# First-layer weights loaded once in 16 rows, and the first chunk joined to the first pair's transfer in a factorization-machine kernel

## The reference

```python
x_reg = input_data @ W_lin.T + b_lin
emb = input_data @ factors
sum_squared = jnp.square(emb.sum(axis=1))
squared_sum = (jnp.square(input_data) @ jnp.square(factors)).sum(axis=1)
h = jax.nn.relu(emb @ W1.T + b1)          # 16 -> 128
h = jax.nn.relu(h @ W2.T + b2)            # 128 -> 64
dnn_out = h @ W3.T + b3                   # 64 -> 1
x = x_reg + 0.5 * (sum_squared - squared_sum)[:, None] + dnn_out
x = 0.5 + jax.nn.sigmoid(x) * 5.0
```

## Time and profile before

| | us |
|---|---|
| median of 3 runs (lowest, highest) | 133.63 (133.58, 133.83) |
| the profiled execution | 133.64 |
| its span, first to last instruction | 131.8 |
| TensorE matmul busy | 107.9 (82%) |
| ScalarE busy | 61.4 (47%) |
| VectorE busy | 52.6 (40%) |
| mean DMA rate over the span | 397 GB/s |

### The profile page before, as it was taken

The page is one execution under the profiler, slowest core; times in us unless marked ns, Lnnn a source line. Parts: engine busy times, 40 slices in busy tenths (PEclk is TensorE's granted clock), DMA queues, the critical chain, the costliest instruction groups (busy, mean ns, idle before and its releaser), DMA issues.

```text
span 131.8 us, 2604 instructions
## 1 busy us (share of the span) xinstructions
PE 107.9 (82%) x1123; PEld 34.9 (26%) x1123; DVE 52.6 (40%) x51; ACT 61.4 (47%) x52; POOL 17.6 (13%) x48
## 2 busy tenths in 40 slices
PE   6059989439999739969649979999569997989992
PEld 4012222012222112212112233222022222345881
DVE  0391063036036036045045016564065351576571
ACT  4030067039039039049058046867069571465851
POOL 3015000200046200110200110064200400000000
PEclk9999999965899977999986999999999999999999
DMA  4999999999999999999999999999999999999700
GB/s 116 417 519 408 408 457 462 398 408 477 428 408 432 447 427 398 467 437 408 437 447 427 398 467 447 393 437 437 398 413 428 438 415 422 414 405 412 304 25 1
DMA packets 3201, 52.36 MB, mean 397 GB/s; under 512 B 372, under 2 KB 504, under 8 KB 1400
## 3 DMA queue, kind: packets, MB, share of 16 engines
q1 hardware_dynamic: 3192, 52.23, 93.2%
HBM read 52.22 MB, written 0.00 MB: 396 GB/s over the span
## 4 chain that ended last, share of the span: by engine, by line
DMA 53%; PE 42%; SPq 1%; DVE 1%; issue 1%; ACT 1%
DMA xr<-in_x_pairs 37%; PE p_lin L506 36%; DMA xr<-in_x_end 16%; PE p_sq L506 2%; PE p_h L600 2%; PE p_tot L506 1%; PE p_h L631 1%; DVE h L454 0%; DVE h L449 0%; PE p_tot L613 0%; SPq L273 0%; SPq L267 0%; SPq L266 0%; ACT lin L341 0%; PE p_tot L620 0%
## 5 line engine op out<-in xcount | busy, mean ns | idle before, releaser
L327 ACT ACTIVATE sq<-xr 128x2560 f32<-128x2560 f32 x20 | 45.8, 2332 | 45.6 <-DMA xr<-in_x_pairs 42.7
L427 DVE TENSOR_TENSOR sq<-xr 128x1536 f32<-128x1536 f32 x20 | 34.6, 1765 | 53.4 <-DMA xr<-in_x_pairs 48.8
L506 PE MATMUL p_lin<-xr,wr 128*17 128x512 f32 x320 | 42.4, 674 | 13.6 <-DMA xr<-in_x_pairs 13.6
L506 PE MATMUL p_lin<-sq,wz 128*18 128x512 f32 x320 | 36.5, 592 | 0.0
L506 PEld LDWEIGHTS p_lin<-xr,wr 128*17 128x17 f32 x320 | 9.6, 107 | 44.3 <-issue 37.6
L307 POOL COPY wr<-hd 128x136 f32 (+1 forms) x20 | 9.6, 482 | 77.8 <-PE p_lin L506 77.8
L506 PEld LDWEIGHTS p_lin<-sq,wz 128*18 128x18 f32 x320 | 9.9, 98 | 24.8 <-issue 24.7
L506 PE MATMUL p_lin<-xr,hd 128*17 128x352 f32 (+1 forms) x128 | 10.0, 380 | 1.3 <-DMA xr<-in_x_end 1.3
L506 PE MATMUL p_lin<-x_one,hd 32*17 32x256 f32 (+1 forms) x28 | 6.1, 654 | 4.4 <-DMA x_one<-in_x_first 4.4
L437 DVE TENSOR_TENSOR sq<-xr 128x1408 f32<-128x1408 f32 (+3 forms) x6 | 6.6, 1134 | 6.1 <-DMA xr<-in_x_end 6.1
L337 ACT ACTIVATE sq<-xr 128x1408 f32<-128x1408 f32 (+3 forms) x6 | 5.7, 982 | 6.3 <-DMA xr<-in_x_end 6.3
(11 more groups left out here) (50 smaller groups left out, 39.5 us busy)
## 6 DMA issues: line engine op xcount, KB each, us to landing
xr<-in_x_pairs SPq DMA_DIRECT2D x9, 4096.0 KB, 21.9
xr<-in_x_groups SPq DMA_DIRECT2D x2, 2048.0 KB, 17.6
xr<-in_x_end SPq DMA_DIRECT2D x1, 2112.0 KB, 17.4
xr<-in_x_end SPq DMA_DIRECT2D x3, 640.0 KB, 19.0
xr<-in_x_end SPq DMA_DIRECT2D x1, 1760.0 KB, 21.2
xr<-in_x_end SPq DMA_DIRECT2D x1, 1056.0 KB, 16.2
hd<-in_head SPq DMA_DIRECT2D x1, 952.0 KB, 4.8
x_one<-in_x_first SPq DMA_DIRECT2D x1, 896.0 KB, 6.6
```

The costliest lines, as they stand in the source:

```text
L327: nc.scalar.activation(sq[:, ring(s), BY_DVE:CHUNKS, :], xr[:, s, BY_DVE:CHUNKS, :], ACT.Square).then_inc(act_squared, 1)
L427: nc.vector.tensor_tensor(sq[:, ring(s), 0:BY_DVE, :], xr[:, s, 0:BY_DVE, :], xr[:, s, 0:BY_DVE, :], ALU.mult).then_inc(dve_squared, 1)
L506: return nc.tensor.matmul(out, lhsT, rhs, start=False, stop=False, skip_group_check=True)
```

## The change

W1 no longer stands in hd: hd's parameter part loses 128 columns (512 bytes in each of 128 rows, 64 KB). A new input w1_once of 16 rows by 256 columns (16 KB) carries W1 transposed beside four identity blocks; one matmul spreads it over the four quarters into a PSUM bank, VectorE copies it into a tile w1, and the first layer reads that. Its transfer stands second in SP's queue.

Chunk 0, the remainder and the first pair now lie side by side in one tile x_all and come in one transfer (39,936 bytes a row), which raises x_landed[0]. All that waited for first_landed now waits for x_landed[0].

Waits: in groups 12 to 17 ScalarE and VectorE wait for a pair's landing once, and not again for its second group (six waits left out); rest_copied is waited for ahead of `square_end(7, 1)` and no longer together with p_lin_done[2].

```diff
-C_W1 = 0
-C_W2 = C_W1 + H1
+C_W2 = 0
         hd = sb("hd", [P, HD])
-        x_one = sb("x_one", [P, B + REST_SETS * REST_COLS])
-        xr = sb("xr", [P, SLOTS, CHUNKS, HALF])
+        w1_sel = sb("w1_sel", [EMB, H1 + P])
+        w1 = sb("w1", [P, H1])
+        x_all = sb("x_all", [P, FIRST + SLOTS * CHUNKS * HALF])
...
             sp.dma_start(hd[:, :], head).then_inc(hd_landed, 16)
-            sp.dma_start(x_one[:, :], x_first).then_inc(first_landed, 16)
-            for p in range(PAIRED // TWO):
+            sp.dma_start(w1_sel[:, :], w1_once).then_inc(w1_landed, 16)
+            sp.dma_start(x_all[:, 0:FIRST + TWO * CHUNKS * HALF], x_first[:, 0:FIRST + TWO * CHUNKS * HALF]
+                         ).then_inc(x_landed[0], 16)
+            for p in range(1, PAIRED // TWO):
...
-            act.wait_ge(first_landed, 16)
+            act.wait_ge(x_landed[0], 16)
             nc.scalar.activation(sqf[:, :], xf[:, :], ACT.Square).then_inc(first_squared, 1)
...
             for g in range(GROUPS, PAIRED):
-                landed(act, g // SLOTS, g % SLOTS)
+                if g % TWO == 0:
+                    landed(act, g // SLOTS, g % SLOTS)
...
-            dve.wait_ge(first_landed, 16)
+            dve.wait_ge(x_landed[0], 16)
             nc.vector.tensor_tensor(sql[:, :, :], xl[:, :, :], xl[:, :, :], ALU.mult).then_inc(rest_squared, 1)
...
+            dve.wait_ge(w1_done, 1)
+            nc.vector.tensor_copy(w1[:, :], p_h1[0][:, 0:H1]).then_inc(w1_ready, 1)
             dve.wait_ge(p_h1_done[0], 2)
...
             for g in range(GROUPS, PAIRED):
-                landed(dve, g // SLOTS, g % SLOTS)
+                if g % TWO == 0:
+                    landed(dve, g // SLOTS, g % SLOTS)
...
             square_end(7, 0)
+
+            dve.wait_ge(rest_copied, 1)
             square_end(7, 1)
-            dve.wait_ge(rest_copied, 1)
             copy_block(2)
...
             pe.wait_ge(hd_landed, 16)
-            pe.wait_ge(first_landed, 16)
+            pe.wait_ge(x_landed[0], 16)
...
             remainder(WZ, ws[:, ENDS + 1:, :], sql)
+            pe.wait_ge(w1_landed, 16)
+            nc.tensor.matmul(p_h1[0][:, 0:H1], w1_sel[:, H1:H1 + P], w1_sel[:, 0:H1],
+                             start=True, stop=True, skip_group_check=True).then_inc(w1_done, 1)
...
-                    mm = nc.tensor.matmul(bank[32 * t:32 * t + 32, 0:n], pr[:, C_W1 + 32 * t:C_W1 + 32 * t + 32], rhs,
+                    mm = nc.tensor.matmul(bank[32 * t:32 * t + 32, 0:n], w1[:, 32 * t:32 * t + 32], rhs,
...
+            pe.wait_ge(w1_ready, 1)
             layer1(0)
```

More of the change, by code:

```diff
@@ L45 @@
 REST_COLS = B // (P // REST_K)
+FIRST = B + REST_SETS * REST_COLS
 BY_DVE = 3
@@ L83, with fm_kernel @@
 HD = HD_L + REST_SETS * LIN
-def fm_kernel(nc, head, x_first, x_pairs, x_groups, x_end, out):
+def fm_kernel(nc, head, w1_once, x_first, x_pairs, x_groups, x_end, out):
     with ExitStack() as ctx:
@@ L120, in fm_kernel @@
         warm = sb("warm", [P, 1])
-        xf = x_one[:, 0:B]
-        xl = x_one[:, B:].rearrange("p (c b) -> p c b", b=REST_COLS)
+        xf = x_all[:, 0:B]
+        xl = x_all[:, B:FIRST].rearrange("p (c b) -> p c b", b=REST_COLS)
+        xr = x_all[:, FIRST:].rearrange("p (s c b) -> p s c b", s=SLOTS, c=CHUNKS)
         w = hd[:, 0:HD_P].rearrange("p (c k) -> p c k", k=LIN)
@@ L135, in fm_kernel @@
         hd_landed = sem("hd_landed")
-        first_landed = sem("first_landed")
+        w1_landed = sem("w1_landed")
+        w1_done = sem("w1_done")
+        w1_ready = sem("w1_ready")
         x_landed = [sem(f"x_landed{t}") for t in range(SLOTS // TWO)]
@@ L273, in _ @@
                 sp.dma_start(xr[:, at:at + TWO].rearrange("p s c b -> p (s c b)"),
-                             x_pairs[p, :, 0:TWO * CHUNKS * HALF]).then_inc(x_landed[at // TWO], 16)
+                             x_pairs[p - 1, :, 0:TWO * CHUNKS * HALF]).then_inc(x_landed[at // TWO], 16)
             for g in range(PAIRED, TOTAL):
@@ L726 @@
     x_rest = rest.reshape(REST_SETS, REST_K, P // REST_K, REST_COLS).transpose(2, 1, 0, 3).reshape(P, -1)
-    x_first = np.concatenate([xT[:P], x_rest], axis=1)
     chunks = xT[P + REST:].reshape(ALL - 1, P, B)
@@ L738 @@
             x_groups[g - PAIRED, :, :CHUNKS * HALF] = rows
+    x_first = np.concatenate([xT[:P], x_rest, x_pairs[0]], axis=1)
+    x_pairs = np.ascontiguousarray(x_pairs[1:])
     ends = chunks[ALL - 1 - ENDS:]
@@ L749 @@
     params = head[:, HD_P:HD_L]
+    w1_once = np.zeros((EMB, H1 + P), f32)
+    w1_once[:, :H1] = np.asarray(L0_rec_W1).T
     for t in range(4):
-        params[32 * t:32 * t + EMB, C_W1:C_W1 + H1] = np.asarray(L0_rec_W1).T
+        w1_once[:, H1 + 32 * t:H1 + 32 * t + EMB] = np.eye(EMB, dtype=f32)
         params[32 * t:32 * t + EMB, C_SE] = 1.0
@@ L761 @@
     params[:, C_B3] = np.asarray(L0_rec_b3)
-    arrays = {"head": head, "x_first": x_first, "x_pairs": x_pairs, "x_groups": x_groups, "x_end": x_end}
+    arrays = {"head": head, "w1_once": w1_once, "x_first": x_first, "x_pairs": x_pairs, "x_groups": x_groups, "x_end": x_end}
     nc = bacc.Bacc("TRN2", target_bir_lowering=False, num_devices=1)
```

## The result

The changed kernel took 135.11 us in the median of 22 runs (133.64 to 137.04), the kernel before 133.65 us (133.50 to 133.83, 22 runs). I had forecast 133.42. The fastest executions equal those of before; the others lie anywhere up to 3.4 us above. The ratio, 1.0039 with a 95% interval of 1.0025 to 1.0054, leaves out executions more than 1.5% above the fastest, which are 10 of the 22 here, so it tells the smaller part of the loss. What has to be explained is a scatter that before does not have. (In the changed kernel line 518 is the matmul in `add_mm`, 506 before, and line 280 the issue of a pair, 273 before. The views leave digits out of names, so w1_sel stands there as w_sel.)

A forecast was written before the change was run, and what follows sets the result against it. The stream of transfers was taken to bound the kernel. From 133.64 us, 0.14 less for the stream and 0.07 less for the moved wait made 133.43, forecast as 133.42; own range 133.25 to 133.6, 8 in 10 within 133.1 to 133.9.

The forecast's parts named there:

- Bound: Whole kernel: the stream of transfers sets the time to the last byte; a microsecond less there is one less overall.
- landings: Pairs on the DMA stream: landed at 17.59, 28.52 and 38.24 us before; merged transfer expected at 17.45.
- code packets: DMA engines: an instruction packet holds up one of 16 by about 1.2 us; a pair lands with the slowest.
- The start: Chunk 0's work waits for the merged transfer at 17.45 us; pair 0 used up at 34.0 at the latest.
- The queue stays full, by 0.6 to 1.9 us: At pair 3's issue: data flow at 35.0 to 36.3 us, before pair 2 is done at 36.9 to 38.1.
- The delay costs 0: After the later start: TensorE finishes pair 2 at 48.2 us, against pair 3 landing at about 48.1.
- a dip of the share: Sign against the forecast: the DMA share dips between 34 and 38 us.
- Rival 1: At pair 3: pair 0 used up later than about 35.5 us, the queue runs dry, likelier 133.9 us; chance 0.08.
- the 16-row transfer: W1's new transfer in SP's queue: costs 0.03 us of stream, bounds 0 to 0.06, the queue behind it being full.
- rival 3: W1's small transfer holds the DMA engines up for up to 1 us, 134.2 at half of that; chance 0.04.
- The bytes: Head of the stream: hd loses 64 KB, w1_once adds 16, so 0.11 us less stream.
- The moved wait: VectorE's addition for block 2 at the end: a single wait saves 0.07 us, bounds 0 and 0.10.

The follow-up runs named there:

- after_delay: Changed kernel with eight more matmuls of 512 columns on TensorE ahead of the W1 matmul: 135.45 us, ratio 1.0131.
- issue_late: Kernel before, with SP issuing pair 3 only when three groups are used up, not two: 135.98 us, ratio 1.0148.
- merge_warm: Kernel before with the merged transfer, the seven wait changes and 60 matmuls of zeros, W1 left in the head: 133.58 us, ratio 0.9998.
- swap_warm: Changed kernel with W1's transfer behind the merged one and 60 matmuls of zeros while TensorE waits: 133.70 us, ratio 0.9995.
- lighter: Changed kernel without the squared products of chunk 0 and the remainder, W1's transfer still ahead: 134.49 us, ratio 1.0039.
- swap: Changed kernel with the merged transfer second in SP's queue and W1's third: 134.45 us, ratio 1.0057.
- merge_18: Kernel before with the merged transfer, issued only after GpSimd's two fills (about 1.8 us), no short transfer ahead: 133.73 us, ratio 1.0017.
- merge_only: Kernel before with chunk 0, the remainder and the first pair in one transfer, W1 still in the head: 133.92 us, ratio 1.0017.
- late_start: Kernel before, transfers untouched, but ScalarE, VectorE and TensorE wait for the first pair before touching chunk 0: 134.68 us, ratio 1.0078.
- merge_twice: Kernel before with only the merged transfer, W1 still in the head, a repeat of merge_only: 133.69 us, ratio 1.0012.
- after_again: Changed kernel unchanged, timed once more: 134.81 us (133.62 to 136.73), ratio 1.0043.
- after_warm: Changed kernel with 50 matmuls of zeros while TensorE waits for the first transfer: 133.97 us, ratio 1.0029.
- split: Changed kernel with chunk 0 and the remainder in their own transfer again, W1's transfer still second: 133.84 us, ratio 1.0015.
- split_swap: Changed kernel with chunk 0 and the remainder in their own transfer, issued second, W1's third: 133.69 us, ratio 1.0004.
- waits_only: Kernel before with only the seven waits changed: 133.69 us, ratio 0.9998.

## Why the prediction was wrong

- **Bound, landings, code packets**: right. What pair 3's landing lost in after_delay and issue_late, 1.1 and 2.3 us, is in the time in full.
- **The start**: the mechanism was right and its numbers too. I had the merged transfer at 17.45 us and pair 0 used up by 34.0 at the latest; the changed kernel's two profiles have 17.51 and 17.52, and issues of pair 3 at 32.94 and 33.95.
- **The step that failed** is the one after it: "The queue stays full, by 0.6 to 1.9 us", from which "The delay costs 0" follows. I let data flow until 36.9 us and took 1 to 2.3 us from issue to data, so that only an issue later than about 35.5 would cost. All profiles that bear on it, in us:

| | pair 3 issued | pair 2 lands | pair 3 lands | execution |
|---|---|---|---|---|
| before | 24.73 | 38.24 | 48.12 | 133.64 |
| merge_warm | 31.15 | 38.16 | 47.94 | 133.64 |
| swap_warm | 32.24 | 38.14 | 48.15 | 133.77 |
| lighter | 32.33 | 38.90 | 48.79 | 134.54 |
| changed | 32.94 | 38.52 | 48.23 | 133.79 |
| swap | 33.15 | 38.04 | 48.11 | 133.75 |
| merge_18 | 33.18 | 38.45 | 48.17 | 133.86 |
| merge_only | 33.25 | 38.16 | 48.41 | 134.07 |
| late_start | 33.52 | 38.31 | 48.47 | 134.54 |
| merge_twice | 33.77 | 38.21 | 47.95 | 133.52 |
| after_again | 33.95 | 38.47 | 48.62 | 134.88 |
| after_warm | 35.57 | 38.33 | 50.19 | 135.83 |
| after_delay | 35.74 | 38.29 | 49.20 | 135.00 |
| issue_late | 36.84 | 38.48 | 50.46 | 136.12 |

  Up to 33.2 us the issue costs nothing clear (lighter's landings are all late, from the merged transfer on). From 33.25 to 33.95, up to 5 us before pair 2 has landed, it costs between nothing (merge_twice) and 0.5 us. Beyond 35.5 it costs 1.1 to 2.3. So there is no single edge at 35.5, and the loss begins some 2 us earlier.
- **Why the margin was wrong.** It was worked out from 36.9, when the slower of the engines that no code packet held up are done with pair 2; by the landings' records the first of the 16 is done at 36.0 to 36.4. That is not enough: data came 0.95 us after the issue in after_delay and issue_late, so by that an issue at 33.95 was still in time for every engine. What the sum had at nothing is that the first packets of a late transfer are slow. By the packets' records those of 32 KB around 36 us took 2.0 to 2.4 us in three cases in after_again and 1.7 to 2.2 in fourteen in after_delay, 1.21 otherwise, and in merge_twice none did. In after_delay the DMA share stayed at 0.99 while the rate fell, so the sign that I had named, a dip of the share, did not come there (in issue_late it did). Why the first packets are slow stays open. Rival 1, at 0.08, had the late issue but as a queue that runs dry.
- **What this explains of the changed kernel.** Its issue falls between 32.9 and 34 us, where the loss begins, and the rise of the clock decides where. That gives up to 0.5 us. The 10 of 22 executions at 135.8 us and above need more: a merged transfer that lands late as well, as in after_warm, a further hit at the end, as in after_again, or something that no profile shows. So the late issue is shown to cost (issue_late) and the late start to scatter (late_start); that they make up the whole loss is not shown.
- **A part of the sum that I had at 0.03 us**, the 16-row transfer, goes with a landing of the long transfer behind it that is late by over a microsecond in some executions (18.57 and 18.83 us, where the others have 17.35 to 17.68; in split 8.93 against 7.67). My reason, the full queue behind it, does not hold for the place that it has, at 1.2 us, when head's data still fill the queue alone; that this is the reason is not shown. This was rival 3, at 0.04. Where a late landing makes the issue later still, both add up: 135.83 us in after_warm's profile.
- **The bytes**: never arrived. With W1 out of the head and its transfer third, swap_warm and split_swap stand at 0.9995 and 1.0004. The head is 64 KB shorter, and VectorE's first operation on it starts at 5.41 to 5.67 us in the nine profiles with the short head and at 5.44 to 5.61 in the eight with the long one:

```profile
5.49 1.78 DVE L418 SCALAR_TENSOR_TENSOR fsq<-hd 128x1552 f32<-128x1552 f32 x1 [4.35 <-DMA hd<-in_head]
```

  (swap_warm). A landing is that of the slowest of 16 engines. By its landings' records eleven engines had their share of the head by 5.0 us and five at 5.4 to 5.5, and at the very end the fastest engine is done 0.17 us earlier than before, the slowest at the same time (126.35 and 126.31). Why five are late I don't know.
- **The moved wait**: the hand-over was sized rightly. The addition follows its product by 0.05 us in the changed kernel and in waits_only, 0.12 before, so it saves 0.07. But in the changed kernel the product itself ends 0.07 later, and in the median of waits_only 0.07 us can't be told from nothing.

What stays open: the longest profile of the changed kernel is of 134.88 us, so its executions up to 137.04 are not explained by any; after_delay, which adds work ahead of pair 0, stays below them, and merge_18 has one of 136.73 without a short transfer.

## What to carry to other kernels

Work that is moved behind a larger transfer does not only start later: follow it to what it frees, and to the issue that waits for that. Where a stream of transfers is the bound, count the margin of an issue from the moment the first DMA engine is done with the transfer ahead, not from its landing; here 3.0 us before that moment cost nothing clear (swap), and 2.9 to 2.2 us up to 0.5 (merge_only, after_again). An edge that one profile just clears will be missed by others, so look at the scatter and not only at the fastest times. Saved bytes count only on the engine that lands last. A short transfer cost nothing measurable behind the first long one (swap_warm, split_swap) and seemed to cost in front of it.

## What the runs showed of the hardware

- A transfer that is queued late is slow even where the engines never stop: in after_delay the DMA share was 0.99 at 279 GB/s between 36 and 38 us, where before has 1.07 at 459. The first packets of 32 KB of pair 3 took 1.7 to 2.2 us each by the packets' records, and 1.21 later on. Why is not shown.
- After an idle stretch of 14.1 us TensorE's granted clock rose to full speed at 20.3 us in one execution of the changed kernel and at 22.5 in another (4.61 and 5.61 us for the same 28 matmuls; 3.31 when it had been kept busy).
- A code packet costs the engine that it falls on 1.2 us of the stream (pair 1 before: fifteen engines by 27.20 us, the last at 28.42), and the first one moves with TensorE's progress: it held up pair 1 before and pair 2 after. The Trainium skill (Runtime: NRT & Kernel Launch, Instruction fetch mechanics) has the cost as mostly hidden; in a stream that never pauses these profiles do not.
